# Scattering the rows of x to expert order instead of their ids, in an attention and mixture-of-experts kernel

## The chip, the cores and the metric

The kernel runs on one core of a Trainium2 chip. The metric is the device time of one execution in microseconds. Three runs of the kernel before took 3083.47, 3100.82 and 3107.78 us; the median is 3100.82 us. The profiled execution took 3095.15 us.

The engines are PE (TensorE, the matmuls), ACT (ScalarE), DVE (VectorE), POOL (GpSimd) and SP (SyncE, which only issues transfers here). Each works through its own instructions in order and waits on semaphores for the others. Indirect transfers are issued from POOL; all other transfers from SP. Both kinds run on the same 16 DMA engines, through different queues (q0 is POOL's, q1 is SP's; q8 and q14 fetch instructions).

## The reference

For x of 4 x 2048 rows of 256 numbers, with xn = layernorm(x):

```python
s = attention(xn)            # 8 heads of 64; one k and one v for all heads; then Wout and a layer norm
g = silu(ffn(xn))            # mixture of 8 experts, each token goes to its 2 best
return x + s * g

# ffn: T = 8192 tokens
logits = x @ wr.T
vals, idx = top_k(logits, 2)
gating = softmax of the two
cap = int(T * 2 // 8 * 1.25)                 # 2560 slots for each expert
pos = cumsum(mask, axis=0) - 1               # place of a token in its expert
dispatch[e, pos] = token, where pos < cap    # other slots hold "no token"
xg = x_pad[dispatch]                         # rows of x in expert order
h = gelu(xg @ w1 + b1);  y = h @ w2 + b2
out = segment_sum(y * gate, dispatch)
```

So before an expert can work, the rows of xn must be brought into the order of its slots. There are 8 x 2560 = 20480 slots, and 16384 pairs of a token and an expert; the slots that are left over stand for no token, and what is computed in them is not used.

## The kernel before

The whole program is one list of slots in time (`slots`). An attention slot ("att", a, b) holds the scores of step a and the weighing of step b = a - 4. A step is one head, 512 queries and 256 keys: four score matmuls on PE (L576), an exponential on ACT over 128 x 1024 numbers (L798), the subtraction that makes the low half of it in bf16 (L1143 on DVE, L1273 on POOL), and 24 matmuls with v on PE (L596, L598, L606). There are 1024 steps: 512, then all expert work (`"turn"`, `"hidden"`, `"second"` slots, 40 groups of 512 expert rows), then the other 512. A group of queries is 64 steps.

Beside this main work each engine runs side chains (Python generators). `clock.at(slot)` places a piece of a side chain in the engine's instruction order at that slot; it is no wait on the chip. An engine whose pieces have nothing to wait for runs ahead of the others.

The pieces that matter here:

- `statistics(g)` in the first attention half: it normalises 512 rows of x, splits them into two f16 halves (`s_hl`), stores them (1 KB a row) in DRAM as `xn_rows`, and turns them for the matmuls. `xT_out` is the buffer of the turned rows; it goes to `xT_rows` in DRAM and is loaded again (L1339 on SP) when k and v of its group are due.
- `route()` on DVE works out for each token and each of its two experts the slot (`scatter_to`, and `gather_from` for the way back). `R_AT` is slot 333.
- `route()` on POOL then scatters token ids: for each of 64 tiles of 128 tokens and each of the two choices one indirect transfer writes 128 numbers of 4 bytes into `slot_token` in DRAM (L1217). `SCATTER_AT` is slot 377, two transfers for every second slot, up to slot 503. Nothing between them waits. Slot 377 holds the scores of step 335; slot 503 those of step 461.
- `load_ids()` on SP brings the ids back in expert order (L1344).
- `gather(fg)` on POOL fetches for each of the 40 groups of expert rows four times 128 rows of 1 KB by their ids out of `xn_rows` (L1265), into `xg`, which PE turns (L621).
- The low half of every fifth step is POOL's (`on_pool`), except between `R_AT` and the end of the scatters, where DVE does all.
- `prepare_q` and `project_out` have small pieces on POOL: a power (L1193) for each tile of 128 queries, and one for each tile of outputs. DVE waits for the first before it can scale q.

## Time and profile before

| | |
|---|---|
| median of 3 runs | 3100.82 us |
| profiled execution, its own time | 3095.15 us |
| its span, first to last instruction | 3093.4 us |
| PE busy | 2880.5 us, 93% |
| DVE busy | 2067.9 us, 67% |
| ACT busy | 1904.6 us, 62% |
| POOL busy | 1156.3 us, 37% |
| mean granted TensorE clock | 0.969 |
| DMA | 138.22 MB, 45 GB/s in the mean |

Busy time is the sum of an engine's instructions; "idle before, releaser" in the rows is the time the engine stood still just ahead of them, put down to the instruction whose semaphore came last. "Issue" is idle time for which the profile shows no wait. The clock is the share of full speed (2.4 GHz) that TensorE was granted. In a row of instruction groups, x124 means 124 instructions, then come their busy time in us and the mean of one in ns.

### The profile page before, as it was taken

To read this page: it belongs to the slowest core of one execution; us is meant where nothing else is said; L and a number is where in the kernel's file an instruction comes from. 1 tells how busy PE (TensorE), PEld (TensorE's weight loads), DVE (VectorE), ACT (ScalarE), POOL (GpSimd) and SP (SyncE) were. 2 spreads that over 40 slices of the span, in tenths; PEclk is the share of its full clock that TensorE was granted. 3 is DMA by queue.
4 is the path that set the end of the run, shared out by engine and by line. 5 is a ranking of instruction groups with operands and counts; after the bars stand their busy time and mean duration, and the time that the engine had idled before them with its cause. 6 is when DMAs were issued, how large, how long until landed. Compare 5 with 4: busy or idle time off the path is not lost.

```text
span 3093.4 us, 86146 instructions
## 1 busy us (share of the span) xinstructions
PE 2880.5 (93%) x38277; PEld 2018.6 (65%) x38277; DVE 2067.9 (67%) x2883; ACT 1904.6 (62%) x2363; POOL 1156.3 (37%) x823
## 2 busy tenths in 40 slices
PE   4999999988778897999999999999989999999996
PEld 3666667666545675666767666677666667666674
DVE  6878888888555674333343334338879999888975
ACT  5666667665544565566565656547666677666764
POOL 2333333323344632221112122104555656565544
PEclk8999999999888998999999999999999999999998
DMA  2111011101100001122122212110111111111101
GB/s 80 36 38 53 26 55 40 41 26 34 38 3 12 6 15 38 64 71 77 55 70 78 71 64 72 51 42 18 34 44 48 46 53 48 46 43 46 36 23 44
DMA packets 91333, 138.22 MB, mean 45 GB/s; under 512 B 15368, under 2 KB 72784, under 8 KB 90960
## 3 DMA queue, kind: packets, MB, share of 16 engines
q1 hardware_dynamic: 73040, 94.86, 9.6%
q0 software_dynamic: 17920, 37.84, 4.4%
q8 instruction: 300, 4.92, 0.7%
q14 instruction: 73, 0.60, 0.1%
HBM read 84.27 MB, written 48.38 MB: 43 GB/s over the span
## 4 chain that ended last, share of the span: by engine, by line
PE 75%; DVE 10%; issue 7%; ACT 5%; POOL 2%; DMA 0%; another core or an unknown queue 0%; SPq 0%; DVEq 0%; POOLq 0%; ACTq 0%
PE pair L576 22%; PE bank L651 14%; PE pair L637 13%; PE bank L598 6%; PE bank L606 6%; PE bank L596 6%; DVE arena L1143 4%; ACT arena L798 3%; PE bank L560 2%; PE bank L519 2%; PE bank L621 1%; POOL w_lo L1245 1%; PE bank L548 1%; PE bank L531 1%; DVE q_n L1066 1%
## 5 line engine op out<-in xcount | busy, mean ns | idle before, releaser
L1143 DVE TENSOR_TENSOR arena<-arena 128x1024 bf16<-128x1024 f32 x854 | 1120.5, 1324 | 345.1 <-ACT arena L798 316.0
L798 ACT ACTIVATE arena<-pair 128x1024 f32<-128x1024 f32 x1024 | 1039.2, 1023 | 482.6 <-PE pair L576 409.5
L576 PE MATMUL pair<-qT,kT 128*128 128x512 f16 x4096 | 1074.9, 385 | 55.7 <-ACT arena L798 48.2
L596 PEld LDWEIGHTS bank<-vhl,arena 128*128 128x128 bf16 x8192 | 595.8, 99 | 147.7 <-issue 30.6
L596 PE MATMUL bank<-vhl,arena 128*128 128x65 bf16 x8192 | 660.8, 194 | 19.9 <-issue 19.8
L598 PE MATMUL bank<-vhl,arena 128*128 128x64 bf16 x8192 | 663.4, 195 | 14.6 <-issue 14.4
L598 PEld LDWEIGHTS bank<-vhl,arena 128*128 128x128 bf16 x8192 | 557.4, 98 | 139.1 <-issue 21.4
L1273 POOL TENSOR_TENSOR arena<-arena 128x1024 bf16<-128x1024 f32 x170 | 351.8, 2069 | 636.2 <-ACT arena L798 628.0
L576 PEld LDWEIGHTS pair<-qT,kT 128*128 128x128 f16 x4096 | 342.9, 99 | 322.5 <-ACT arena L798 56.3
L606 PE MATMUL bank<-vhl,arena 128*128 128x65 bf16 x8192 | 426.5, 194 | 26.9 <-issue 18.7
L651 PE MATMUL bank<-w_hl,arena 128*128 128x256 bf16 x3840 | 425.7, 273 | 0.6 <-DVE att L1159 0.6
L814 ACT ACTIVATE h_f<-pair,b1T 128x512 f32<-128x512 f32 x320 | 219.4, 686 | 333.9 <-PE pair L637 333.9
L651 PEld LDWEIGHTS bank<-w_hl,arena 128*128 128x128 bf16 x3840 | 374.1, 98 | 43.6 <-DVE att L1159 0.8
L1149 DVE TENSOR_TENSOR arena<-h_f,arena 128x512 bf16<-128x512 f32 x320 | 221.6, 692 | 270.4 <-ACT arena L685 269.0
L1265 POOL DMA_INDIRECT att<-xn_rows,slot_ids x160 | 162.1, 1013 | 609.7 <-PE bank L621 571.9
L637 PE MATMUL pair<-kT,w_hi 128*128 128x512 f16 x1280 | 383.4, 381 | 3.3 <-ACT kT L685 3.3
L606 PEld LDWEIGHTS bank<-vhl,arena 128*128 128x128 bf16 x8192 | 324.2, 98 | 33.5 <-issue 24.0
L1159 DVE TENSOR_TENSOR att<-bank,vhl 128x256 f32<-128x256 f32 x160 | 67.8, 424 | 295.8 <-PE bank L651 291.2
L637 PE MATMUL pair<-kT,w_lo 128*128 128x512 f16 x640 | 243.7, 381 | 0.0
L637 PEld LDWEIGHTS pair<-kT,w_hi 128*128 128x128 bf16 x1280 | 125.4, 98 | 146.5 <-issue 3.9
L685 ACT ACTIVATE arena<-h_f 128x512 bf16<-128x512 f32 x320 | 201.9, 631 | 10.2
L1193 POOL TENSOR_TENSOR q_small<-q_small,minus_half 128x8 f32<-128x8 f32 x64 | 155.4, 2428 | 118.9 <-DVE q_small L1062 117.8
(194 smaller groups left out, 2554.5 us busy)
## 6 DMA issues: line engine op xcount, KB each, us to landing
expert_rows<-att SPq DMA_DIRECT2D x40, 512.0 KB, 2.6
raw<-in_L_ffn_w SPq DMA_DIRECT2D x32, 512.0 KB
xn_rows<-s_hl SPq DMA_DIRECT2D x16, 512.0 KB, 2.9
w_lo<-in_L_attn_x SPq DMA_DIRECT2D x64, 128.0 KB
out<-w_lo SPq DMA_DIRECT2D x64, 128.0 KB
s_xin<-in_L_attn_x SPq DMA_DIRECT2D x12, 512.0 KB, 4.6
xT_rows<-xT_out SPq DMA_DIRECT2D x12, 512.0 KB, 2.9
xT<-xT_rows SPq DMA_DIRECT2D x12, 512.0 KB, 4.4
```

The costliest lines, as they stand in the source:

```text
L576: t = nc.tensor.matmul(pairs[n % 2][:, i * BANK:(i + 1) * BANK], kT[b % 2][:, part, kb * P:(kb + 1) * P], qT[g % 2][:, h, :], start=(part ...
L596: nc.tensor.matmul(bank[:, at:at + DH + 1], p_top[:, s, cols, 1], V[:, kb, 0:DH + 1], start=(kb == 0 and qb == 0), stop=False, skip_group_ ...
L598: nc.tensor.matmul(bank[:, at:at + DH], p_top[:, s, cols, 1], V[:, kb, DH + 1:VW], start=False, stop=False, skip_group_check=True)
L606: t = nc.tensor.matmul(bank[:, at:at + DH + 1], p_lo[:, s, cols], V[:, kb, 0:DH + 1], start=False, stop=(kb == KB - 1), skip_group_check=True)
L637: t = nc.tensor.matmul(bank, w[e % 2][:, c, cols], xgT[fg % 2][:, kind, :], start=(n == 0), stop=(n == 3 * DC - 1))
L651: t = nc.tensor.matmul(bank[:, 0:D], h[fg % 2][:, f, cols], w2_hl[e % 2][:, f, at:at + D], start=(f == 0 and h is h_hi and at == 0), stop= ...
L685: return nc.scalar.activation(o, i, ACT.Copy)
L798: nc.scalar.activation(p_f32[:, n % NP, :], pairs[n % 2][:, :], ACT.Exp).then_inc(exped, 1)
L814: nc.scalar.activation(h_f32[k % 2], lent[k % 4], ACT.Gelu_apprx_tanh, bias=b1T[:, e * FC + f:e * FC + f + 1]).then_inc(gelued, 1)
L1143: nc.vector.tensor_tensor(p_lo[:, n % NP, :], p_f32[:, n % NP, :], p_top[:, n % NP, :, 1], ALU.subtract).then_inc(lowed, 1)
L1149: nc.vector.tensor_tensor(h_lo[fg % 2][:, f, :], h_f32[k % 2], h_hi[fg % 2][:, f, :], ALU.subtract).then_inc(h_rest, 1)
L1273: nc.gpsimd.tensor_tensor(p_lo[:, n % NP, :], p_f32[:, n % NP, :], p_top[:, n % NP, :, 1], ALU.subtract).then_inc(lowed_pool, 1)
```

## The change

1. `slot_token` and everything on ids goes: the store of zero ids, 128 scatters of 128 x 4 bytes, `load_ids`, the 160 gathers on POOL.
2. A tensor `routed_rows` in DRAM takes the rows themselves: 20480 slots and 16384 rows behind them for tokens over the capacity, 1 KB each. SP first fills the slots with zeros: 80 stores of 256 KB, one for every third slot from the start of attention (`zero_rows`).
3. For each tile of 128 tokens SP loads its rows from `xn_rows` into one of four buffers of 1 KB a partition, which lie in `xT_out` (`move_rows`, 64 loads of 128 KB), six slots ahead. It waits until both scatters from that buffer four tiles earlier have landed.
4. POOL scatters each tile twice, 128 rows of 1 KB, one transfer for each slot instead of two for each second one. Before each it waits for the exponential of two steps before, `exped >= a - 1` at the slot of step a.
5. For each group of 512 expert rows SP loads 512 KB in one plain transfer (`load_routed`), 4 KB in a row for each partition.

```diff
@@ constants
-                nc.vector.memset(zero_ids[:, :], 0).then_inc(dve_const, 1)
+                nc.vector.memset(h_f32[0], 0.0).then_inc(zero_made, 1)
@@ exponent(n), n == 0
-                    act.wait_ge(ids_zeroed, 16)
@@ route() on POOL
                 for t in range(NT):
-                    yield from clock.at(SCATTER_AT + 2 * t)
-                    pool.wait_ge(routed, N_ROUTE["all"])
-                    pool.wait_ge(ids_zeroed, 16)
                     for k in range(TOP_K):
+                        at = SCATTER_AT + 2 * t + k
+                        yield from clock.at(at)
+                        pool.wait_ge(routed, N_ROUTE["all"])
+                        pool.wait_ge(rows_zeroed, 16 * NZERO)
+                        pool.wait_ge(rows_loaded[t % 4], 16 * (t // 4 + 1))
+                        pool.wait_ge(exped, slots[at][1] - 1)
                         nc.gpsimd.indirect_dma_start(
-                            slot_token, bass.IndirectOffsetOnAxis(scatter_to[k][:, t:t + 1], 0),
-                            token_id[:, t:t + 1], None).then_inc(ids_scattered, 16)
+                            routed_rows, bass.IndirectOffsetOnAxis(scatter_to[k][:, t:t + 1], 0),
+                            moving[t % 4], None).then_inc(rows_scattered[t % 4], 16)
@@ gather(fg) on POOL: gone
-                for j in range(GT):
-                    nc.gpsimd.indirect_dma_start(
-                        xg[i][:, j, :], None, xn_rows,
-                        bass.IndirectOffsetOnAxis(slot_ids[:, e, q * GT + j:q * GT + j + 1], 0)
-                    ).then_inc(x_gathered[i], 16)
@@ SP
+            def zero_rows(i):
+                yield from clock.at(base[0] + 3 * i)
+                sp.wait_ge(zero_made, 1)
+                nc.sync.dma_start(zeroed_rows[i], h_f32[0].bitcast(F16)).then_inc(rows_zeroed, 16)
+
+            def move_rows(t):
+                i = t % 4
+                yield from clock.at(SCATTER_AT + 2 * t - 6)
...
+                sp.wait_ge(rows_scattered[i], 16 * TOP_K * (t // 4))
+                nc.sync.dma_start(moving[i], xn_tiles[t]).then_inc(rows_loaded[i], 16)
+
+            def load_routed(fg):
+                e, q = divmod(fg, NQ)
+                yield from clock.at(experts_at if fg < 2 else place["hidden", fg - 2, FC - 1])
+                for i in range(4):
+                    sp.wait_ge(rows_scattered[i], 16 * TOP_K * NT // 4)
+                sp.wait_ge(o_turned, XG * GT)
+                sp.wait_ge(xg_turned, 2 * (fg - 1))
+                nc.sync.dma_start(xg[fg % 2], routed_tiles[e, :, q * GT:(q + 1) * GT, :]).then_inc(x_gathered[fg % 2], 16)
```

POOL's instructions where the scatters begin, before (`slot_token` takes ids; `half_rstd` and `q_small` are the powers of an output tile and of a query tile; in brackets the semaphores that the instruction waits for):

```order
L1217 DMA slot_token<-token_id,scatter_to 36864x1 [waits ids_zeroed,routed]
L1217 DMA slot_token<-token_id,scatter_to 36864x1 x3
L1193 TENSOR_TENSOR half_rstd<-o_small,minus_half 128x1 [waits o_var]
L1193 TENSOR_TENSOR q_small<-q_small,minus_half 128x8 [waits q_var]
L1217 DMA slot_token<-token_id,scatter_to 36864x1 x16
L1193 TENSOR_TENSOR half_rstd<-o_small,minus_half 128x1 [waits o_var]
```

and now:

```order
L1223 DMA routed_rows<-xT_out,scatter_to 36864x512 [waits rows_loaded0,exped,rows_zeroed,routed]
L1223 DMA routed_rows<-xT_out,scatter_to 36864x512 [waits exped]
L1223 DMA routed_rows<-xT_out,scatter_to 36864x512 [waits exped,rows_loaded1]
L1195 TENSOR_TENSOR half_rstd<-o_small,minus_half 128x1 [waits o_var]
L1223 DMA routed_rows<-xT_out,scatter_to 36864x512 [waits exped]
L1195 TENSOR_TENSOR q_small<-q_small,minus_half 128x8 [waits q_var]
L1223 DMA routed_rows<-xT_out,scatter_to 36864x512 [waits exped,rows_loaded2]
```

Sixteen scatters in a row with no wait among them have become sixteen with a wait ahead of each, and the second power has moved behind one scatter.

SP's instructions in the first attention half, around the first load of turned rows, now (`h_f` is the buffer of zeros; before, the same rows stand there without L1333):

```order
L1316 DMA xT_rows<-xT_out 128x2048 [waits s_turned_copied]
L1333 DMA routed_rows<-h_f 128x1024 x3
L1308 DMA s_xin<-in_L_attn_x 128x4x256
L1333 DMA routed_rows<-h_f 128x1024
L1327 DMA xT<-xT_rows 128x4x512 [waits kv_projected,s_scored,q_projected,xT_stored]
```

Four stores of 256 KB now go out between the store of turned rows and the load that brings them back.

## Rows read from the trace of the kernel before

**Rows 1.** Page: the chain of work that ended last, by engine
```profile
PE 75%; DVE 10%; issue 7%; ACT 5%; POOL 2%; DMA 0%; another core or an unknown queue 0%; SPq 0%; DVEq 0%; POOLq 0%; ACTq 0%
```

**Rows 2.** Busy time by stretch: scatters, after them, experts
```profile
core 0: us, PE busy (x) PEld busy (x) DVE busy (x) ACT busy (x) POOL busy (x), PEclk, DMA share, GB/s
743.00:1075.00 332.00, 270.54 (x3792) 180.04 (x3788) 202.06 (x256) 164.03 (x180) 173.34 (x146) 0.87 0.10 18
1090.00:1170.00 80.00, 79.34 (x1324) 57.12 (x1322) 65.44 (x79) 54.54 (x61) 26.90 (x16) 1.00 0.05 14
1210.00:2030.00 820.00, 816.36 (x6005) 562.05 (x6003) 298.75 (x483) 471.62 (x699) 152.30 (x151) 1.00 0.20 65
```

**Rows 3.** The exponentials in 743:1075, 1090:1170 and 2250:2500, in this order
```profile
L798 ACT ACTIVATE arena<-pair 128x1024 f32<-128x1024 f32 x124 | 126.4, 1024 | 142.3 <-PE pair L576 74.7 <-remote 63.1 <-PE bank L606 3.6
L798 ACT ACTIVATE arena<-pair 128x1024 f32<-128x1024 f32 x43 | 43.7, 1024 | 18.7 <-PE pair L576 18.7
L798 ACT ACTIVATE arena<-pair 128x1024 f32<-128x1024 f32 x124 | 125.5, 1023 | 38.1 <-PE pair L576 37.8
```

**Rows 4.** Busy time: a run of scatters, the gap behind it, slower scatters
```profile
852.00:875.00 23.00, 14.49 (x157) 7.68 (x154) 8.19 (x10) 5.32 (x6) 17.13 (x17) 0.77 0.03 2
875.00:895.00 20.00, 20.00 (x301) 14.11 (x302) 14.16 (x19) 13.47 (x15) 0.85 (x2) 0.93 0.03 9
1004.00:1030.00 26.00, 25.71 (x427) 18.50 (x426) 22.73 (x31) 18.02 (x20) 21.99 (x16) 1.00 0.06 8
```

**Rows 5.** Scatters and exponentials in 852:875, then in 1004:1030
```profile
L1217 POOL DMA_INDIRECT slot_token<-token_id,scatter_to x16 | 16.5, 1033 | 4.8 <-issue 4.8
L798 ACT ACTIVATE arena<-pair 128x1024 f32<-128x1024 f32 x5 | 5.1, 1024 | 10.0 <-remote 6.9 <-PE pair L576 3.1
...
L1217 POOL DMA_INDIRECT slot_token<-token_id,scatter_to x13 | 18.8, 1443 | 3.7 <-issue 3.7
L798 ACT ACTIVATE arena<-pair 128x1024 f32<-128x1024 f32 x14 | 14.2, 1024 | 4.8 <-PE pair L576 4.7
```

**Rows 6.** PE in 743:1075, one group; instruction queue in 852:875, then in 1004:1030
```profile
L606 PE MATMUL bank<-vhl,arena 128*128 128x65 bf16 x992 | 58.8, 198 | 18.7 <-issue 18.7
...
q8 instruction: 2, 0.03, 1.3%
...
q8 instruction: 4, 0.07, 2.5%
```

**Rows 7.** POOL's timeline: start, duration, idle time before
```profile
872.92 0.96 POOL L1217 DMA_INDIRECT slot_token<-token_id,scatter_to  x1 [0.30 <-issue]
...
1073.65 0.96 POOL L1217 DMA_INDIRECT slot_token<-token_id,scatter_to  x1 [0.30 <-issue]
```

**Rows 8.** SP's timeline: loads of turned rows, load of ids, bias
```profile
258.82 0.53 SPq L1339 DMA_DIRECT2D xT<-xT_rows  x1
1080.69 0.37 SPq L1344 DMA_DIRECT2D slot_ids<-slot_token  x1
1182.05 0.81 SPq L1311 DMA_DIRECT2D vhl<-in_L_ffn_b  x2
```

**Rows 9.** POOL's timeline: the fourth gather of the first group
```profile
1184.63 0.95 POOL L1265 DMA_INDIRECT att<-xn_rows,slot_ids  x1 [0.30 <-issue]
```

**Rows 10.** PE's timeline: projection of k and v; first turned expert rows
```profile
266.51 0.27 PE L488 MATMUL bank<-wkv_hi,xT 128*128 128x128 bf16 x2
...
1187.72 1.89 PE L621 MATMUL bank<-ident,att 128*128 128x128 f16 x16 [6.51 <-DMA att<-xn_rows,slot_ids]
```

**Rows 11.** Software queue in 1210:2000: packets, MB, share of 16 engines
```profile
q0 software_dynamic: 7087, 19.39, 8.5%
```

**Rows 12.** Page: transfers by line, KB each, median us to landing
```profile
expert_rows<-att SPq DMA_DIRECT2D x40, 512.0 KB, 2.6
xT<-xT_rows SPq DMA_DIRECT2D x12, 512.0 KB, 4.4
```

**Rows 13.** Page: the gathers, and what POOL waited for ahead of them
```profile
L1265 POOL DMA_INDIRECT att<-xn_rows,slot_ids x160 | 162.1, 1013 | 609.7 <-PE bank L621 571.9
```

More of the change, by code:

```diff
@@ L116, in build_program @@
     xn_groups = xn_rows.rearrange("(g j p) d -> g p j d", j=GT, p=P)
+    NZERO = ROWS // (2 * P)
+    zeroed_rows = routed_rows[0:ROWS, :].rearrange("(i p j) d -> i p (j d)", p=P, j=2)
+    xn_tiles = xn_rows.rearrange("(t p) d -> t p d", p=P)
+    routed_tiles = routed_rows[0:ROWS, :].rearrange("(e p j) d -> e p j d", p=P, j=CT)
     expert_tiles = expert_rows.rearrange("(e p j) d -> e p j d", p=P, j=CT)
@@ L237, in build_program @@
         xT_out = sb("xT_out", [P, 2 * DC, GP], F16)
+        moving = [cut(flat(xT_out, F16), i, [2 * D]) for i in range(4)]
         c_work = [sb(f"c_work{i}", [P, 2 * D], F32) for i in range(2)]
@@ L341, in build_program @@
             "routed", "route_iota", "route_exp", "route_counted")]
-        ids_scattered, ids_zeroed, ids_loaded = sem("ids_scattered"), sem("ids_zeroed"), sem("ids_loaded")
+        rows_zeroed = sem("rows_zeroed")
+        rows_loaded, rows_scattered = [[sem(f"{n}{i}") for i in range(4)] for n in ("rows_loaded", "rows_scattered")]
         b2_loaded = [sem(f"b2_loaded{i}") for i in range(2)]
@@ L427, in statistics @@
                     pe.wait_ge(s_lo, g + 1)
-                    pe.wait_ge(dve_const, 5)
+                    pe.wait_ge(dve_const, 4)
                     view = bank.bitcast(F16)
@@ L461, in route @@
                     pe.wait_ge(*free)
-                pe.wait_ge(dve_const, 5)
+                pe.wait_ge(dve_const, 4)
                 pe.wait_ge(routed, N_ROUTE["mask"])
@@ L1188, in constants @@
                                         pattern=[[1, P]], channel_multiplier=-1).then_inc(pool_const, 1)
-                nc.gpsimd.iota(token_id[:, :], [[P, NT]], base=0, channel_multiplier=1).then_inc(pool_const, 1)
                 yield
@@ L1253, in combine @@
                                         ALU.add).then_inc(c_added, 1)
-            def gather(fg):
-                i = fg % 2
-                yield from clock.at(experts_at if fg < 2 else place["hidden", fg - 2, FC - 1])
-                pool.wait_ge(ids_loaded, 16)
-                for k in range(2):
-                    pool.wait_ge(s_stored[k], 16 * NG // 2)
-                pool.wait_ge(o_turned, XG * GT)
-                pool.wait_ge(xg_turned, 2 * (fg - 1))
-                e, q = divmod(fg, NQ)
-                for j in range(GT):
-                    nc.gpsimd.indirect_dma_start(
-                        xg[i][:, j, :], None, xn_rows,
-                        bass.IndirectOffsetOnAxis(slot_ids[:, e, q * GT + j:q * GT + j + 1], 0)
-                    ).then_inc(x_gathered[i], 16)
             def low(n):
@@ L1281, in _ @@
                 prepare_kv(g) for g in range(NG)] + [prepare_q(t) for t in range(NT)] + [
-                project_out(t) for t in range(NT)] + [combine(t) for t in C_ORDER] + [gather(fg) for fg in range(FG)])
+                project_out(t) for t in range(NT)] + [combine(t) for t in C_ORDER])
         @block.sync
@@ L1339, in prepare_kv @@
                 nc.sync.dma_start(xT[:, :, gi * GP:(gi + 1) * GP], xT_rows[g]).then_inc(xT_loaded, 16)
-            def load_ids():
-                yield from clock.at(SCATTER_AT + 2 * NT)
-                sp.wait_ge(ids_scattered, 16 * NT * TOP_K)
-                nc.sync.dma_start(slot_ids[:, :, :], slot_token[0:ROWS, :].rearrange(
-                    "(e p j) o -> p e (j o)", p=P, j=CT)).then_inc(ids_loaded, 16)
+            def zero_rows(i):
[5 more added lines that the diff above has]
+                yield from clock.at(SCATTER_AT + 2 * t - 6)
+                sp.wait_ge(xT_stored, 16 * (NG - BG))
+                for k in range(2):
+                    sp.wait_ge(s_stored[k], 16 * NG // 2)
+                sp.wait_ge(s_scored, NG)
+                sp.wait_ge(rows_scattered[i], 16 * TOP_K * (t // 4))
[8 more added lines that the diff above has]
+                nc.sync.dma_start(xg[fg % 2], routed_tiles[e, :, q * GT:(q + 1) * GT, :]).then_inc(x_gathered[fg % 2], 16)
             def project_out(t_id):
@@ L1379, in _ @@
                 weights(p) for p in range(NPIECE)] + [bias(e) for e in range(E)] + [prepare_kv(g) for g in range(NG)] + [
-                load_ids()] + [project_out(t) for t in range(NT)] + [store_rows(fg) for fg in range(FG)] + [
+                zero_rows(i) for i in range(NZERO)] + [move_rows(t) for t in range(NT)] + [load_routed(fg) for fg in range(FG)] + [project_out(t) for t in range(NT)] + [store_rows(fg) for fg in range(FG)] + [
                 combine(t) for t in C_ORDER])
```

14 lines of the change are left out of this document (4 added, 10 removed).

## The prediction

> **What bounds the kernel now.** I read the chain of waits first: PE carries 75% of it, DMA under 1% [rows 1]. Whatever the change does must be seen in PE's time. Then I cut the span into stretches, to see where PE is not full [rows 2]. In the expert stretch it is busy for 816.36 of 820 us at full clock. Right behind the scatters, from 1090 to 1170, it is busy for 79.34 of 80. Between 743 and 1075, the time of the 128 scatters of ids, it is busy for 270.54 of 332, at a granted clock of 0.87 (part of the time it stood at the lower of its two levels, 1.2 instead of 2.4 GHz), and the DMA share is small (0.10). That is the one bad stretch that the change touches.
>
> To price it I count steps by their exponentials [rows 3]: 124 in 332 us, so 2.68 us a step; 43 in 80 us behind the scatters, 1.86 us; 124 in 250 us in the second half, 2.02 us, with the same side work on queries and outputs and the combination of the results besides. The stretch of the scatters is 332 - 124 x 1.86 = 101 us longer than by the one rate, 332 - 124 x 2.02 = 82 us longer than by the other.
>
> What takes them? A cut inside the stretch tells [rows 4, 5]. From 852 to 875 sixteen scatters stand nearly back to back (1.03 us each, 0.30 us apart) and PE is busy for 14.49 of 23 us, clock 0.77, five exponentials begin; from 875 to 895 POOL is idle but for two powers, PE is busy for 20.00 of 20. From 1004 to 1030 there are thirteen scatters and three powers, each scatter 1.44 us long and again some 0.30 us behind the last, so one in 1.74 us, and PE is busy for 25.71 of 26 us with fourteen exponentials: 1.86 us a step. So scatters do not hurt as such. They hurt at one in 1.3 us and do not at one in 1.74. In the hurt stretches PE waits for nobody that the profile names ("issue", 18.7 us in one group alone), and two packets of instructions arrive in 23 us where four arrive in 26 [rows 6]. I read this as PE short of instructions because the DMA engines are held by the scatters, though their recorded share of time is 3%.
>
> The landing supports it. The last scatter starts at 1073.65 and takes 0.96 us [rows 7]; SP, which waits for all of them, issues its load at 1080.69 [rows 8]: 6.1 us behind the last issue. The fourth gather of 128 rows of 1 KB starts at 1184.63 and takes 0.95 us [rows 9], and PE has its data at 1187.72 [rows 10]: 2.1 us. If the run ahead of the last scatter was like that of sixteen above, a backlog of 6.1 - 2.1 = 4 us over it means that a scatter of 128 x 4 bytes takes the DMA engines about (16 x 1.33 + 4) / 16 = 1.6 us. This estimate lies between the two spacings, as it should.
>
> Every scatter in the trace is one of 4 bytes, so it cannot tell size from pace; the change alters both. A rule of the Trainium skill speaks against my reading (page "Runtime: NRT & Kernel Launch", Instruction fetch mechanics): fetching a block of instructions costs one tail bump, "mostly hidden". Taken at its word nothing would be lost to fetching, and the sum below would lose its one gain and end at 3105. The idle time in 852 to 875 speaks for the loss.
>
> **The change part by part.**
>
> *Scatters, size and pace.* The window begins at slot 377 as before and holds 128 slots. Each scatter waits for the exponential of two steps before, so no more than one goes out for each slot, except where POOL catches up behind a power. At 1.86 to 2.02 us a slot this is the harmless spacing. The row that shows a scatter beside a full PE has POOL at 21.99 of 26 us, so POOL holds the pace with little to spare: sixteen slots at 1.95 us give 31 us, sixteen scatters at 1.44 + 0.30 and one pair of powers (some 3 us) 31 us. DVE does every low half there, and was busy for 22.73 of 26 us; it holds too. I take 1.95 us a step, between the rate behind the scatters and that of the second half: 124 x 1.95 = 242, **-90 us** (ends -101 and -82 from the two rates; 0 if nothing is cured).
>
> *Bytes.* In the expert stretch the software queue takes 8.5% of 16 engines over 790 us, 67 us, for 160 gathers less a few: 0.44 us of all engines for 128 KB [rows 11]. Here 128 scatters and 64 loads of 128 KB come to 192 x 0.44 = 84 us, a third of the window, where ids took next to nothing. No stretch of attention shows this share beside a full PE. Below nothing there is no reason for it; above, a third of the time in which a fetch stands behind a row. I take **+5 us**, ends 0 and 45 (the end is a step of 2.3 us, halfway back to 2.68).
>
> *POOL's order.* The power of a query tile now stands among paced scatters, one of them ahead of it, and DVE needs it three slots later. If POOL is a slot or two late, DVE waits, and its low halves with it. Eight tiles at 0 to 1.5 us: **+3 us**, ends 0 and 12.
>
> *SP.* `move_rows` waits for a landing. A scatter issued at T has landed by T + 2.1 as the gather did, the load of 128 KB should take no longer than the 2.6 us of a 512 KB store [rows 12], and the buffer is due six slots later, 11 us: it holds. Behind that wait stand seven loads of expert weights and two of turned rows. SP lags by about two slots; ACT meets the weights four slots behind their place, the turned rows are due three behind. Taken with the zeros.
>
> *Zeros.* 80 stores of 256 KB, 21 MB, in the first 240 slots. By the store of 512 KB in 2.6 us each has passed in under 2 us, so they are cheap beside 480 us. What they delay is the load of turned rows: four stores go out ahead of the first. In the second group SP issued that load at 258.82 [rows 8], it lands in 4.4 us [rows 12], and PE projects at 266.51 [rows 10]: 3.3 us to spare, against 1 MB ahead, some 3 to 5 us. Four such loads, and two in the scatter window: **+2 us**, ends 0 and 12.
>
> *Gathers.* 160 instructions of 1.01 us go from POOL, but POOL stood idle for 571.9 us ahead of them, waiting for PE [rows 13], and PE was full: nothing, hidden under PE's matmuls in 1210 to 2030. At the first group PE waited 6.51 us for the gathers, until 1187.72. Now the load stands on SP behind the two bias loads, which wait for the last weighing: they were issued at 1182.05 and take 0.81 us [rows 8], the load lands 4.4 us later, so 1187.3: **0**, ends -2 and +3. Later groups are issued a whole group ahead.
>
> *Start.* The memset on DVE grows from 160 to 512 columns, one iota goes: under 0.5 us, with the wait of ACT for the zero ids going too. **0.**
>
> Sum: 3093.4 - 90 + 5 + 3 + 2 = 3013.4; the profiled execution's own time is 1.75 above its span: **3015 us**. The profiled execution (3095.15) lies 5.7 under the median of the runs, so a median of three may well come out at 3020.
>
> **The rivals.**
>
> *The bytes take part of it back (0.18).* Rows of 1 KB on a third of the engines' time starve PE as ids did at a faster pace, only less: 2.2 to 2.4 us a step. At 2.3 it is 124 x 2.3 = 285, saving 47; with +5 for the rest 3093.4 - 47 + 5 + 1.75 = 3053. Against it: the expert stretch has a DMA share of 0.20 and no loss, but a PE that asks for far fewer instructions (6005 matmuls in 820 us against 1324 in 80). The Trainium skill has a rule for it (page "DMA: Bandwidth & Descriptors", Queues, rings and completion order): each DMA engine changes between queues only behind a whole packet, so longer packets hold an instruction fetch longer. It is why this rival has the chance that it has.
>
> *It isn't the scatters that starve PE, or an indirect transfer does so whatever its size (0.11).* The window stays at 2.68 us a step, one scatter for each slot being more than it bears; 3095 + 10 = 3105. For it: nothing in the trace shows 1 KB rows beside attention at this rate. Against it: the rows of 1004 to 1030.
>
> *The scatters become the bound (0.09), slower than before.* A scatter of 128 rows into scattered places of DRAM may take longer than a slot. Then `move_rows` waits for it, POOL for the load, the query power stands behind POOL's wait, DVE behind the power with every low half, and PE behind DVE. The window is then 128 times a scatter. It decides from 332 / 128 = 2.6 us each; at 3.0 us the window takes 384 us, +52, with +7 for the rest 3154. Against it: 0.44 us of engine time for the same bytes the other way, and writes of rows land in 2.6 us for four times as much. For it: nothing in the trace writes rows to scattered places of DRAM.
>
> **How the numbers follow.** My forecast has 0.62, ends 3093.4 + 1.75 - 101 = 2994 and 3095 - 82 + 5 + 12 + 12 + 3 = 3045. With the first rival up to 3062, 8 in 10 are inside. Range **2994 to 3062**. About 1%, 31 us, is what this measurement can tell: the runs lie 24 us apart. Faster by over that is below 3070: 0.62 + 0.18 = 0.80. Same: the second rival, 0.11. Slower: the third, 0.09.
>
> **What would show it.** Right: the stretch from 743 on takes about 240 us for 124 exponentials, PE without "issue" idle time and at full clock; scatters some 1.9 us apart; the expert stretch still 820 us; the first group of expert rows at the same distance from the last weighing. Wrong: "issue" on PE in the window (first or second rival); DVE waiting for POOL's `q_small`, POOL for SP's loads (third); PE waiting for `xT` in the first half (zeros).

## The result and the profile after

The changed kernel takes 3019.27 us (median of four runs, 3014.99 to 3022.14), the kernel before 3104.30 us in the same session (3083.47 to 3111.84): a ratio of 0.9735, 95% interval 0.9685 to 0.9786. The profiled execution has a span of 3020.4 us against 3093.4, so 73 us are to be accounted for; 80 were forecast.

The chain of waits of the changed kernel still stands on PE, as before [rows 1]:

```profile
PE 77%; DVE 10%; issue 6%; ACT 5%; POOL 2%; DMA 1%; SPq 0%; DVEq 0%; ACTq 0%; POOLq 0%
```

Windows of the changed kernel, cut at the first scatter (743), behind the last one (1008) and at the end of the first attention half (1106). The cuts at 1134 and 1954 are those of the expert stretch in [rows 2], 76 us earlier. Columns: stretch, length, busy time of PE, PE's weight loads, DVE, ACT, POOL, then granted clock, DMA share, GB/s:

```profile
0.00:743.00 743.00, 669.99 (x10768) 478.81 (x10769) 606.63 (x966) 489.32 (x554) 236.20 (x137) 0.97 0.21 72
743.00:1008.00 265.00, 249.64 (x3896) 173.82 (x3894) 205.03 (x262) 167.97 (x185) 200.74 (x146) 0.97 0.34 114
1008.00:1106.00 98.00, 97.34 (x1631) 70.65 (x1630) 76.09 (x93) 64.58 (x71) 30.45 (x19) 0.99 0.04 13
1106.00:1134.00 28.00, 17.44 (x116) 9.61 (x112) 8.37 (x16) 15.72 (x22) 0.55 (x1) 0.81 0.25 75
1134.00:1954.00 820.00, 816.92 (x6000) 562.25 (x6001) 298.54 (x484) 471.25 (x699) 1.62 (x3) 1.00 0.20 65
1954.00:2177.00 223.00, 220.33 (x3164) 155.78 (x3163) 156.47 (x185) 144.25 (x175) 84.07 (x47) 1.00 0.10 31
```

Against [rows 2] the gain is all in one place. The scatters run from 743 to 1008 instead of to 1075, with the granted clock at 0.97 instead of 0.87. The end of the first half moves from 1182 to 1106: 363 us from the cut instead of 439, 76 less. The kernel before, over its 439 us and over the 223 us behind its expert stretch:

```profile
743.00:1182.00 439.00, 375.46 (x5550) 256.36 (x5545) 283.41 (x355) 233.68 (x256) 204.83 (x165) 0.90 0.09 16
2030.00:2253.00 223.00, 220.36 (x3165) 155.78 (x3164) 156.44 (x185) 144.28 (x176) 84.15 (x47) 1.00 0.10 31
```

Of the 76 us, 48 are idle time of PE that is gone (63.5 us there, 16.0 now), and 28 are the same matmuls taking less time at a higher clock (375.46 us busy there, 346.98 now). The expert stretch is 820 us again, although its 160 gathers on POOL are gone (POOL 1.62 us busy). The first 743 us are as long as before, with 21 MB of zeros written in them. So is the start of the second half: 223 us for the same work in both. The last 3 us, 76 - 3 = 73, are given back further on in the second half, which I can't explain and which is less than the runs lie apart.

But PE isn't full among the scatters: 249.64 of 265. In the list of groups, here of the exponentials alone between 743 and 1008 (busy, mean ns, idle time before them and its releasers), there are 128 of them, 2.07 us a step where I had forecast 1.95:

```profile
L801 ACT ACTIVATE arena<-pair 128x1024 f32<-128x1024 f32 x128 | 130.0, 1023 | 67.5 <-PE pair L580 46.3 <-remote 19.5 <-issue 1.5
```

Where the rest is lost shows in three short windows of the changed kernel and in POOL's timeline beside them (start, length, and idle time before with its releaser):

```profile
808.00:825.00 17.00, 17.00 (x271) 11.93 (x270) 16.32 (x22) 10.23 (x12) 14.60 (x11) 1.00 0.31 103
825.00:840.00 15.00, 11.02 (x117) 6.57 (x115) 5.98 (x7) 5.85 (x6) 9.77 (x9) 0.78 0.35 122
840.00:856.00 16.00, 16.00 (x256) 11.38 (x254) 11.80 (x16) 9.98 (x12) 10.34 (x8) 0.99 0.22 77
```

```profile
818.23 1.88 POOL L1195 TENSOR_TENSOR q_small<-q_small,minus_half 128x8 f32<-128x8 f32 x1
820.31 1.47 POOL L1223 DMA_INDIRECT routed_rows<-xT_out,scatter_to  x1 [0.20 <-issue]
822.08 0.96 POOL L1223 DMA_INDIRECT routed_rows<-xT_out,scatter_to  x1 [0.30 <-issue]
823.35 1.19 POOL L1223 DMA_INDIRECT routed_rows<-xT_out,scatter_to  x1 [0.30 <-issue]
...
833.28 0.96 POOL L1223 DMA_INDIRECT routed_rows<-xT_out,scatter_to  x1 [0.30 <-issue]
834.77 1.33 POOL L1223 DMA_INDIRECT routed_rows<-xT_out,scatter_to  x1 [0.53 <-issue]
838.98 1.81 POOL L1223 DMA_INDIRECT routed_rows<-xT_out,scatter_to  x1 [2.87 <-ACT arena L801]
```

Behind the power of a query tile POOL is several slots late. None of the next eleven scatters has an exponential to wait for, so each starts 0.30 us behind the end of the last, as before the change (0.20 ahead of the first, 0.53 ahead of the last); only at 838.98 is POOL held again (2.87 us, by ACT). Some four scatters into the run PE begins to miss time, 4 us of the 15 from 825 to 840. The pace is a lower bound on the place of a scatter, and no bound on the distance between two of them.

### The profile page after: what moved, and what is told of

Its sections match the earlier page's. It is cut to its first block, busy times and chain, and to the rows that moved or that the text cites. A ratio compares the mean times of both kernels' runs of the same rounds, so it can differ in the third digit from the quotient of the medians.

```text
span 3020.4 us, 86225 instructions
## 1 busy us (share of the span) xinstructions
PE 2855.9 (95%) x38277; PEld 2008.6 (67%) x38277; DVE 2066.3 (68%) x2883; ACT 1903.8 (63%) x2363; POOL 1021.0 (34%) x662
## 4 chain that ended last, share of the span: by engine, by line
PE 77%; DVE 10%; issue 6%; ACT 5%; POOL 2%; DMA 1%; SPq 0%; DVEq 0%; ACTq 0%; POOLq 0%
PE pair L580 22%; PE bank L655 14%; PE pair L641 14%; PE bank L602 6%; PE bank L610 6%; PE bank L600 6%; DVE arena L1146 4%; ACT arena L801 3%; PE bank L564 2%; PE bank L523 2%; PE bank L625 1%; POOL w_lo L1251 1%; PE bank L552 1%; PE bank L535 1%; DVE q_n L1069 1%
## 5 line engine op out<-in xcount | busy, mean ns | idle before, releaser
L602 PE MATMUL bank<-vhl,arena 128*128 128x64 bf16 x8192 | 655.8, 195 | 2.1 <-issue 1.8
L600 PE MATMUL bank<-vhl,arena 128*128 128x65 bf16 x8192 | 653.6, 193 | 3.4 <-issue 2.8
L610 PE MATMUL bank<-vhl,arena 128*128 128x65 bf16 x8192 | 421.8, 194 | 13.4 <-POOL arena L1264 8.0
L1223 POOL DMA_INDIRECT routed_rows<-xT_out,scatter_to x128 | 171.9, 1343 | 65.5 <-issue 33.8
```

The costliest lines, as they stand in the source:

```text
L600: nc.tensor.matmul(bank[:, at:at + DH + 1], p_top[:, s, cols, 1], V[:, kb, 0:DH + 1], start=(kb == 0 and qb == 0), stop=False, skip_group_ ...
L602: nc.tensor.matmul(bank[:, at:at + DH], p_top[:, s, cols, 1], V[:, kb, DH + 1:VW], start=False, stop=False, skip_group_check=True)
L610: t = nc.tensor.matmul(bank[:, at:at + DH + 1], p_lo[:, s, cols], V[:, kb, 0:DH + 1], start=False, stop=(kb == KB - 1), skip_group_check=True)
```

## The experiments

All verdicts below go by two things: the span of the profiled execution, and PE's idle time with the releaser "issue" (it waits for no engine and no transfer) summed over its groups between 743 and 1060. Of the changed kernel that sum is 14.5 us, of the kernel before 55.3. Where a kernel was run several times, the ratio to the kernel before is given with its interval. A span is one execution: those of the kernel before lie up to 34 us apart over all its runs (3083.47 to 3117.31), those of the others up to 14. A difference to the one span of 3093.4 is good to some 10 us, not to the tenth that is written.

### Which of the two changes cures it: pace or size

**ids_paced**: the kernel before, with the pace alone. Ids of 4 bytes, one scatter for each slot.

```diff
                     for k in range(TOP_K):
+                        at = SCATTER_AT + 2 * t + k
+                        yield from clock.at(at)
...
+                        pool.wait_ge(exped, slots[at][1] - 1)
```

> The kernel before, with ids of 4 bytes as before, but one scatter for each slot and the wait for the exponential of two steps before ahead of each. Theory pace (indirect transfers that follow one another in 1.3 us leave PE short of instructions, whatever their size): the gain of the change comes back without its rows, 3010 to 3025 us, with short runs of scatters and idle time put down to issue only where POOL catches up. Theory size (a scatter of 4 bytes holds the DMA engines, one of 1 KB does not): most of the loss stays, 3075 to 3100 us.

Measured: 3046.89 us, ratio 0.9844 (0.9805 to 0.9883), span 3040.5, "issue" 27.0 us. The pace alone brings 52.9 us of 73, neither all nor none: the time lies between the two that were expected.

**rows_unpaced**: the changed kernel, with the size alone. Rows of 1 KB, both scatters of a pair at one slot, no wait on exponentials. SP loads only the first four tiles of rows, so 60 of the 64 loads of 128 KB are missing and the rows that are scattered are not the tokens'.

```diff
-                        at = SCATTER_AT + 2 * t + k
+                        at = SCATTER_AT + 2 * t
-                        pool.wait_ge(rows_loaded[t % 4], 16 * (t // 4 + 1))
-                        pool.wait_ge(exped, slots[at][1] - 1)
+                        for i in range(4):
+                            pool.wait_ge(rows_loaded[i], 16)
```

> The changed kernel with scatters of 1 KB rows two for every second slot and no wait between them, as the ids went before; the loads are left out but for the first four tiles, so the scattered data is not the tokens'. Theory pace: the stretch from 743 to the last scatter takes about 330 us again, the whole 3080 to 3110 us. Theory size: about 240 to 265 us, the whole 2995 to 3025 us.

Measured: 3072.78 us, span 3071.1, "issue" 42.1 us. The size alone brings 22.3 us, again between the two expected times. Two windows of this kernel, the second in the midst of a run of scatters:

```profile
743.00:1060.00 317.00, 273.69 (x3859) 183.84 (x3858) 204.01 (x259) 167.24 (x184) 182.61 (x146) 0.87 0.19 71
868.00:884.00 16.00, 6.59 (x46) 2.92 (x46) 3.13 (x4) 2.05 (x2) 11.41 (x12) 0.68 0.26 103
```

The clock stands at 0.87 as before, and in sixteen microseconds with rows going out back to back PE starts 46 matmuls.

**no_scatter**: the floor. The kernel before with no scatters at all.

```diff
-                for t in range(NT):
...
+                yield
```

> The kernel before with the 128 scatters of ids left out, so all slots name token 0. The floor of both theories: from 743 on 1.86 to 1.95 us a step, the whole 2993 to 3008 us. If a third thing takes the time (DVE doing all low halves, the expert weights), the stretch stays above 2.0 us a step and the whole above 3015 us.

Measured: 2991.71 us, span 2989.9, "issue" 0.0 us, clock 1.00 between 743 and 1060. So 128 scatters of ids cost 103.5 us, 0.81 us each; the prediction had worked out 101 from [rows 3] by the rate right behind the scatters. The floor is one execution, and it is good to about 3 us: its first expert group waits 9.57 us for the gathers, where [rows 10] have 6.51. By that floor the changed kernel has 30.5 us left to gain.

With both edits the four spans form a table: ids 3093.4 and paced 3040.5, rows 3071.1 and paced 3020.4. The pace is worth 53 us with ids and 51 with rows, the size 22 and 20. The two add up: of the 73 us some 52 are the pace's and 21 the size's. The size's part is no more than twice what one span can tell; that it comes out alike in both columns, and that "issue" falls with it (55.3 to 42.1, 27.0 to 14.5), is what speaks for it.

### Where the last 30 us are

**rows_spread**: the changed kernel with a scatter in three of four slots.

```diff
+    def scatter_at(t, k):
+        return SCATTER_AT + 4 * (2 * t + k) // 3
...
-                        at = SCATTER_AT + 2 * t + k
+                        at = scatter_at(t, k)
```

> The changed kernel with the scatters four slots for three of them apart (1.33 slots each), so that POOL has spare time behind its powers and need not catch up; DVE does the low halves alone for 42 slots more. Theory pace: the six short stretches of idle PE that are left in the changed kernel go, 3000 to 3012 us. Theory size or bytes: the bytes are the same, 3015 to 3025 us.

Measured: 3020.39 us, ratio 0.975 (0.9715 to 0.9786), span 3017.1, "issue" 13.9 us: no gain, and the expectation that a wider pace would relieve PE is missed. POOL's timeline of this kernel says why:

```profile
846.44 2.56 POOL L1198 TENSOR_TENSOR q_small<-q_small,minus_half 128x8 f32<-128x8 f32 x1 [2.53 <-DVE q_small L1068]
849.18 1.04 POOL L1226 DMA_INDIRECT routed_rows<-xT_out,scatter_to  x1 [0.18 <-ACT arena L804]
850.53 0.96 POOL L1226 DMA_INDIRECT routed_rows<-xT_out,scatter_to  x1 [0.30 <-issue]
851.79 1.16 POOL L1226 DMA_INDIRECT routed_rows<-xT_out,scatter_to  x1 [0.30 <-issue]
853.26 0.96 POOL L1226 DMA_INDIRECT routed_rows<-xT_out,scatter_to  x1 [0.30 <-issue]
854.52 1.28 POOL L1226 DMA_INDIRECT routed_rows<-xT_out,scatter_to  x1 [0.30 <-issue]
```

The powers come late by what POOL waits for DVE ahead of them (2.01 us for the first, 2.53 for the second), not by what scatters take. A power makes POOL some four slots late however far apart the scatters are planned, and five of them follow at 1.3 us. PE's gaps begin at 853.42.

**rows_gapped**: no scatter in four slots that begin just ahead of a query tile's powers and end two behind them; the sixteen slots of a tile keep twelve.

```diff
+    free_slots = [s for s in range(SCATTER_AT, CUT + PRE) if not 1 <= (s - PRE) % 16 <= 4]
+
+    def scatter_at(t, k):
+        return free_slots[2 * t + k]
```

> The changed kernel with the scatters one for each slot, but none in the four slots of every sixteen in which POOL stands before and in its two powers, so that it never has scatters to catch up; they end at slot 548 instead of 504. Theory catch-up (what is left of the loss comes from the four to ten scatters that follow one another in 1.3 us behind the powers): 2993 to 3005 us, 15 to 25 below the changed kernel. Theory toll (each scatter of rows costs PE 0.2 us wherever it stands): 3015 to 3022 us.

Measured: 3003.56 us, ratio 0.9701 (0.9664 to 0.9739), span 3002.9, "issue" 6.5 us. It has as many scatters in as many slots as rows_spread and is 14.2 us shorter in span; only their places differ. This confirms the catch-up runs as the cause of 17.5 us of the changed kernel's 30.5, as was expected. Its window:

```profile
743.00:1060.00 317.00, 309.05 (x5023) 219.58 (x5021) 260.51 (x336) 214.64 (x240) 201.59 (x144) 1.00 0.28 96
```

**ids_gapped**: the same places, ids of 4 bytes.

```diff
                     for k in range(TOP_K):
-                        at = SCATTER_AT + 2 * t + k
+                        at = scatter_at(t, k)
```

> The kernel before, ids of 4 bytes, scatters placed as in rows_gapped with the same wait. Theory catch-up: 2993 to 3010 us, and the rows in the transfers of the change bring nothing of their own. Theory toll: 128 times the 0.4 us that the paced ids cost, 3035 to 3050 us.

Measured: 3022.05 us, ratio 0.9764 (0.9724 to 0.9804), span 3021.1, "issue" 15.3 us. So rows remain 18 us better than ids in the same places, and neither theory had that number. Most of it comes from the stretch of the scatters: the last exponential of the first half starts 29.5 us later than in no_scatter with ids and 14.3 us later with rows. A scatter of ids costs 0.24 us here (31.2 us over the floor). A kernel that only paces the ids and spares those places isn't told apart from the changed kernel (3022 and 3019), and does without zeros, moves and rows in DRAM.

**gapped_early_load**: rows_gapped, with the load of the first expert rows ahead of the two bias loads on SP.

```diff
-                weights(p) for p in range(NPIECE)] + [bias(e) for e in range(E)] + [prepare_kv(g) for g in range(NG)] + [
+                weights(p) for p in range(NPIECE)] + [load_routed(fg) for fg in range(FG)] + [bias(e) for e in range(E)] + [prepare_kv(g) for g in range(NG)] + [
```

> rows_gapped with the loads of the first two groups of expert rows ahead of the two bias loads on SP, which wait for the last weighing. In rows_gapped PE waits some 7 us for the first group there. If that wait is only the load's own 4.4 us behind a late issue, it goes but for a rest: 2996 to 3001 us against 3003.6, the fastest of all. If something else orders the first turn (the last output tile, ACT's table), no change, 3002 to 3006 us.

Measured: 3000.46 us (six runs), ratio 0.9692 (0.9657 to 0.9728), span 2996.6. The first turn of expert rows in the changed kernel, and in this one (PE's timeline; in brackets the wait):

```profile
1113.44 1.35 PE L625 MATMUL bank<-ident,att 128*128 128x128 f16 x11 [6.98 <-DMA att<-routed_rows]
```

```profile
1091.50 1.78 PE L630 MATMUL bank<-ident,att 128*128 128x128 f16 x15 [4.09 <-DMA att<-routed_rows]
```

The wait is 2.9 us shorter than in the changed kernel and 3.2 us shorter than in rows_gapped (7.33); it was expected to go but for a rest, and 4.09 us are left. Against rows_gapped the total isn't told apart, the intervals overlap; it is the fastest kernel of the study, 6.7 us above the floor.

### What starves PE

My reading ahead of the runs, called supply here, was that PE's instructions arrive late while the DMA engines are held by small transfers. Its rivals: that the indirection matters, or the making of descriptors on POOL, or that PE itself runs slower beside scatters.

**expert_extra**: the kernel before with eight scatters of 4 bytes behind every gather group, 320 in all, in the stretch where PE needs far fewer instructions. Their results are used by nothing.

```diff
+                for j in range(8):
+                    m = 8 * fg + j
+                    nc.gpsimd.indirect_dma_start(
+                        spare[m // NT], bass.IndirectOffsetOnAxis(token_id[:, m % NT:m % NT + 1], 0),
+                        token_id[:, m % NT:m % NT + 1], None).then_inc(spare_done, 16)
```

> The kernel before with 8 more scatters of 128 x 4 bytes behind the four gathers of each group of expert rows, 320 in all, to places that nothing reads. Theory supply (transfers in a row slow only how fast PE gets instructions, to about 17 in a us; the experts ask for 15, attention for 40): the 820 us of the expert stretch grow by less than 20 us. Theory machine (they slow PE's work or its semaphores whatever it runs): the bursts fill 15 of every 20 us, and as in the stretch of the scatters about 0.6 of their time is lost, the stretch grows by over 200 us.

Measured: 3366.65 us, span 3364.9: 271.5 us more, 0.85 us for each scatter. Supply had been given under 20, a slowing of PE itself over 200: the number fell to the other side. Windows of this kernel: four gathers and then four small scatters of a run begun at 1345.22, what follows them, late in the run begun at 1291.76, right behind that run, and a stretch without any:

```profile
1345.22:1350.27 5.05, 5.05 (x49) 4.52 (x47) 1.12 (x2) 2.04 (x3) 3.83 (x4) 1.00 0.27 78
1350.27:1354.70 4.43, 4.43 (x42) 3.79 (x39) 0.42 (x1) 0.00 (x0) 3.52 (x4) 1.00 0.16 34
1355.00:1360.00 5.00, 2.51 (x10) 1.10 (x11) 0.00 (x0) 0.00 (x0) 3.78 (x5) 0.79 0.02 0
1310.00:1322.00 12.00, 3.66 (x11) 0.89 (x10) 0.00 (x0) 0.00 (x0) 9.26 (x10) 0.50 0.41 41
1326.00:1334.00 8.00, 7.91 (x51) 6.08 (x52) 1.06 (x4) 0.00 (x0) 0.00 (x0) 0.71 0.00 0
1330.00:1345.00 15.00, 15.00 (x98) 8.82 (x97) 5.69 (x9) 9.72 (x16) 0.00 (x0) 0.98 0.09 36
```

The same in the kernel before: from the first scatter of a run to PE's first gap, the rest of the run, and a piece of it:

```profile
852.78:856.60 3.82, 3.82 (x66) 2.61 (x63) 3.50 (x5) 1.39 (x2) 3.16 (x3) 1.00 0.01 0
857.00:875.00 18.00, 9.77 (x77) 4.49 (x78) 4.28 (x4) 2.83 (x4) 13.22 (x13) 0.70 0.03 1
868.00:872.00 4.00, 1.37 (x12) 0.79 (x12) 0.00 (x0) 0.00 (x0) 3.08 (x4) 0.50 0.02 0
```

and PE's first gaps, in the kernel before and in this one:

```profile
856.95 0.19 PE L598 MATMUL bank<-vhl,arena 128*128 128x64 bf16 x1 [0.28 <-issue]
1355.14 0.50 PE L653 MATMUL bank<-w_hl,arena 128*128 128x256 bf16 x3 [0.38 <-issue]
```

Gathers leave PE full: four in a row here, and 160 of them in the full expert stretch of [rows 2]. Counted from the first scatter, the first gap comes after 3.9 us in attention (three scatters, 129 matmuls and loads) and after 4.5 us in the experts (four scatters, 81). That is nearer to equal in time than in instructions. Behind it PE gets 155 instructions in 18 us in attention (8.6 in a microsecond) and 21 in 12 us in the experts (1.8). A stock of instructions that runs out and a fixed rate of supply would give equal counts, and these are not. In the experts the single matmuls come in a beat of 0.7 us (PE's timeline):

```profile
1309.44 0.38 PE L653 MATMUL bank<-w_hl,arena 128*128 128x256 bf16 x1 [1.02 <-issue]
1310.16 0.37 PE L653 MATMUL bank<-w_hl,arena 128*128 128x256 bf16 x1 [0.33 <-issue]
1310.86 0.37 PE L653 MATMUL bank<-w_hl,arena 128*128 128x256 bf16 x1 [0.33 <-issue]
1311.57 0.60 PE L653 MATMUL bank<-w_hl,arena 128*128 128x256 bf16 x2 [0.34 <-issue]
```

The trace can also be asked for the instructions themselves. The page of this kernel has 300 packets on the instruction queue q8, for 76,554 matmuls and weight loads of PE: one packet for some 255 of them. Between 1296.5 and 1334 the only queue that moved anything was POOL's; q8 brought nothing. Yet in that time PE starves until 1321, waits 5.03 us for DVE, and from 1326.09 runs 48 matmuls without a gap (the page's row, the DMA view of 1296.5 to 1334, PE's timeline):

```profile
q8 instruction: 300, 4.92, 0.7%
q0 software_dynamic: 773, 0.69, 20.3%
1326.09 7.60 PE L653 MATMUL bank<-w_hl,arena 128*128 128x256 bf16 x48 [5.03 <-DVE att L1161]
```

By this record, if q8 is all that brings them, the instructions that PE ran from 1326 on had been brought before 1296.5, and lay ready while it starved. So supply fails in the form that the prediction gave it: PE is not waiting for a fetch over the DMA engines. The reading of [rows 6], two packets of instructions in 23 us against four in 26, took an effect for a cause: PE ran 311 and 853 instructions there, and at 255 a packet that is 1.2 and 3.3 packets. The expectation was off in its rates too: [rows 4] give 13.5 instructions in a microsecond for the bad stretch, not 17, and [rows 2] 33 for attention, not 40. That PE itself, or what hands it its next instruction, is slowed beside small transfers is not ruled out by any run here, and its number was the one that came. Which of these it is stays open: the record says "issue" and no more.

**plain_pool**: 128 plain transfers on POOL, each of 128 pieces of 4 bytes, in place of the scatters; token numbers are stored straight in order.

```diff
-                        nc.gpsimd.indirect_dma_start(
...
+                        nc.gpsimd.dma_start(
+                            slot_token[(TOP_K * t + k) * P:(TOP_K * t + k + 1) * P, :],
+                            token_id[:, t:t + 1]).then_inc(ids_scattered, 16)
```

> The kernel before with each scatter of ids made a plain transfer of the same 128 x 4 bytes from POOL to consecutive places, unpaced as before (so the ids are not in expert order). If it is the indirection: about the floor, 2990 to 3005 us. If any transfer that POOL makes descriptors for does it: 3070 to 3100 us.

Measured: 3024.08 us, span 3022.3, "issue" 13.0 us: 32.4 above the floor, between the two expected numbers. The indirection isn't needed for a loss, but 71 of the 103.5 us come only with it. POOL spends 0.54 us on a plain transfer and 0.96 and more on an indirect one, so the runs are shorter too; which of the two makes the difference wasn't tried. POOL's timeline shows sixteen at once, 0.54 us each:

```profile
866.38 8.56 POOL L1217 DMA_DIRECT2D slot_token<-token_id  x16
```

**sp_small**: the same 128 stores from SP's queue, none from POOL.

```diff
+            def small_stores(t):
+                yield from clock.at(SCATTER_AT + 2 * t)
...
+                    nc.sync.dma_start(slot_token[at:at + P, :], token_id[:, t:t + 1]).then_inc(ids_scattered, 16)
```

> The kernel before with no scatters from POOL; instead SP stores the same 128 x 4 bytes to consecutive places, 128 times, two for every second slot without a wait, 0.4 to 0.6 us apart (so the ids are not in expert order). Theory engines (small pieces in the DMA engines hold up the fetching of instructions, whoever makes the descriptors): as the plain transfers from POOL, 3015 to 3035 us. Theory POOL (it is the making of descriptors on POOL): the floor, 2988 to 3000 us.

Measured: 3019.57 us, span 3017.8, "issue" 14.3 us. That is inside what was expected if the issuing engine doesn't matter. It costs what plain_pool costs (27.9 and 32.4 above the floor, one execution each) with POOL free of it, 44.89 us busy between 743 and 1060. So for plain transfers it is neither POOL nor its descriptors: they starve PE whichever of the two engines issues them. For the 71 us that only the indirect ones cost, POOL's part is not excluded, since no other engine issued those.

### Bytes

**narrow256** and **narrow512**: rows_gapped, but only the first 256 or 512 bytes of each row are scattered, to a tensor of rows of that width; the experts read rows that were never written.

```diff
+    narrow_rows = nc.dram_tensor("narrow_rows", [ROWS + TOP_K * T, 128], F16).ap()
...
-                            moving[t % 4], None).then_inc(rows_scattered[t % 4], 16)
+                            moving[t % 4][:, 0:128], None).then_inc(rows_scattered[t % 4], 16)
```

> rows_gapped with only the first 256 bytes of each row scattered, to a tensor of its own that nothing reads; loads and zeros as there. Theory small writes (below 512 bytes a write costs more, as the Trainium skill has it on its page DMA: Bandwidth & Descriptors, Specifications): as the ids in the same places, 3015 to 3025 us. Theory packets or bytes (the fewer bytes the less): at most rows_gapped's 3003.6, 2998 to 3004 us.

> The same with the first 512 bytes of each row. By both theories as rows_gapped or just under, 2998 to 3005 us; only if each step down in size costs something is it between 3005 and 3015 us.

Measured: 3005.63 us, ratio 0.9704 (0.9646 to 0.9762), and 3006.37 us, ratio 0.9707 (0.9649 to 0.9764); "issue" 6.5 and 7.0 us, as with full rows (6.5). Between 256 bytes and 1 KB a scatter costs the same to some 3 us in 128 of them, so the bytes of a scatter cost nothing that these runs can tell. Neither expected range of narrow256 was met: 3005.63 lies 1.6 us above the one by bytes and 9 below the one by small writes; 3006.37 lies 1.4 us above the 3005 of narrow512, which is no more than the two executions of each lie apart. The 64 loads of full rows were kept in both, and no run varied them alone. The Trainium skill (page "DMA: Bandwidth & Descriptors", Specifications) names 512 bytes as the least transfer for full rate, with a read-modify-write below it; at 256 these runs show no cost of it. Why 4 bytes cost 18 us more stays open. The ids go to a target of 147 KB, the narrow rows to one of at least 9 MB, and nothing between 4 and 256 bytes was run.

## Why the prediction held, and where it didn't

- **The window: right in place and in the part of pace, 15 us too good.** Forecast 332 - 90 us for 124 steps; measured 265 x 124 / 128 = 257, so -75, outside the term's own ends of -101 and -82. The cause was right as far as it says that scatters at one in 1.3 us cost PE its time; size has a part of its own, some 21 us, that the term didn't hold. "No more than one goes out for each slot, except where POOL catches up behind a power" names the exception and prices it at nothing. It is the term that was mis-sized: rows_gapped, which takes those runs away, gets 17.5 us of span back. The way to see it was there: the wait counts exponentials, so a late POOL finds all its waits met. With POOL held for DVE ahead of both powers and busy in both, four or more slots pass, and four or more scatters follow at 1.3 us, the rate that [rows 4] show to be harmful. The sum of sixteen slots had the pair of powers at 3 us and no wait ahead of them; in rows_spread POOL waited 2.01 and 2.53 us there.
- **Why PE starves: not as read.** The prediction had PE short of instructions because the scatters hold the DMA engines. The sum didn't use it, since the harmful and the harmless spacing came from [rows 4, 5] directly; that is why the forecast survives it. The instruction queue brought nothing for 37 us in which PE first starved and then ran full.
- **The price of the loss: right.** 101 us by the rate behind the scatters, 103.5 by the kernel without them.
- **Bytes, +5: wrong in kind for the scatters, small in size.** Rows at a quarter of their width take as long. The rival of 3053 rested on bytes, and no run gives it ground; the loads' part was not tried. The Trainium skill (page "DMA: Bandwidth & Descriptors", Queues, rings and completion order) says that a DMA engine changes queues only behind a whole packet. What the prediction drew from it, that longer rows cost PE more, isn't borne out between 256 bytes and 1 KB, and the 4-byte ids were the dearer ones.
- **POOL's order, +3: the right place, the wrong mechanism.** DVE doesn't wait for the late power: the group of `q_n`, which needs `q_small`, has 0.0 us of idle time ahead of it between 743 and 1008 (row below). PE starves behind the power. This and the window's -90 are one term: forecast -90 + 5 + 3 = -82, measured -76. That the total is off by only 4 us is in part luck: 10 us of costs that didn't come as forecast stood against a window 15 us too good.

```profile
L1069 DVE TENSOR_TENSOR q_n<-q_f,q_small 128x512 f32<-128x512 f32 x8 | 5.5, 684 | 0.0
```

- **Zeros and SP, +2: nothing.** The first scatter starts at 742.94, before the change at 743.40.
- **Gathers, 0: right.** 820 us in both, POOL's 160 instructions gone.
- **First turn, 0: right.** The wait is 6.98 us where it was 6.51 [rows 10]. What was not seen is that the two bias loads ahead of it could be passed, for 2.9 us.
- **The scatters as bound: did not come.** They keep up, and SP's loads too. Ahead of the scatters POOL waits for ACT and DVE, and for no load (the group between 743 and 1008):

```profile
L1223 POOL DMA_INDIRECT routed_rows<-xT_out,scatter_to x128 | 171.9, 1343 | 65.5 <-issue 33.8 <-DVE gather_from L1023 19.2 <-ACT arena L801 12.5
```

- **Any indirect transfer starves PE whatever its size: four fifths true of scatters (81.2 of 103.5 us).** That is what unpaced rows kept. The rival's other half, that it isn't the scatters, is refuted by the kernel without them. The prediction gave this rival the whole gain to lose, because it didn't let pace act alone; its own [rows 4] had shown that pace acts.
- **The rule that fetching instructions is mostly hidden** (the Trainium skill, page "Runtime: NRT & Kernel Launch", Instruction fetch mechanics): the traces don't speak against it. Without scatters there are 0.0 us of "issue", and in expert_extra PE starved and recovered without a packet of instructions between. What failed is the time that the prediction drew from it, 3105, which is 86 us too long: a hidden fetch doesn't mean that nothing is lost.

What stays open: by what path small transfers starve PE; why 4 bytes are dearer than 256; the last 6.7 us above the floor; and the estimate that one scatter holds the DMA engines for 1.6 us. No run was made for that estimate, and ids_gapped speaks against it. There the last six scatters are issued from 1082.24 to 1092.03, so at 1.6 us each no backlog is left, and SP should go 2.1 us behind the last; it goes 4.2 us behind (POOL's and SP's timeline):

```profile
1090.60 1.43 POOL L1224 DMA_INDIRECT slot_token<-token_id,scatter_to  x1 [0.30 <-issue]
1096.19 0.37 SPq L1351 DMA_DIRECT2D slot_ids<-slot_token  x1
```

## What to carry to other kernels

Where the busiest engine shows idle time with no releaser, look at what the DMA queues issue at that moment by count and by distance, not by bytes or by recorded share. Spread small transfers, and make the pace a distance: a wait on another engine's progress is only a lower bound, and behind anything that holds the issuing engine all the delayed ones go out at once, so leave free slots there. Before turning data into larger pieces, try the pace alone: here it gave 53 of 73 us with a few lines, and with gaps 72. And before idle time without a releaser is given a cause, count what the suspected queue carried in it: here the instruction queue brought nothing, and PE ran full behind the run of transfers all the same.

## What the runs showed of the hardware

- A run of small transfers costs PE time, issued by POOL or by SP. Per transfer of 128 pieces over the floor: 0.81 us for ids scattered unpaced (103.5 / 128), 0.63 for rows of 1 KB unpaced, 0.24 for rows at one a slot, 0.10 with gaps at the powers; 0.40 and 0.24 for ids in the same two places; 0.25 and 0.22 for plain stores of 128 x 4 bytes from POOL and from SP.
- PE's first gap comes 3.9 us behind the first scatter of an unpaced run in attention (129 instructions) and 4.5 us in the experts (81). Then matmuls come in a beat of some 0.7 us, singly or in twos in the experts, until about the end of the run. Gathers of 1 KB rows, four in a row, leave PE full.
- The instruction queue q8 brings a packet for some 255 instructions of PE, and it isn't what PE waits for while it starves: nothing came on q8 from 1296.5 to 1334, while PE starved and then ran 48 matmuls without a gap.
- In starved stretches the granted clock falls to 0.50 to 0.79, part or all of the time at 1.2 instead of 2.4 GHz. In rows_gapped it is 1.00 from 743 to 1060, with the scatters still there.
- Width between 256 bytes and 1 KB had no effect beyond 3 us on 128 scatters (3005.63, 3006.37 and 3003.56 us).
